# Projecting before the normalisation in two graph convolutions: a column-sum correction for the mean, the row scale in the adjacency matrix

## Chip, core and metric

The kernel runs on one NeuronCore of a Trainium2 chip, in fp32 with some bf16 helpers. The metric is the device time of one launch in microseconds (us), the median of several runs. TensorE is called PE, VectorE DVE, ScalarE ACT, GpSimd POOL and SyncE SP, as in the profile.

## What is computed

Four graph layers on 64 nodes with 768 features and 1024 edges, each added to its input and followed by a LayerNorm over the features. The second and the fourth are the ones that matter here.

```
def _layernorm(x, eps=1e-05):            # over the 768 features of a node
    m = mean(x); v = var(x)
    return (x - m) / sqrt(v + eps)

x = _layernorm(x + L0(x))                # two relational convolutions, each with a gate over 512 query rows
x = _layernorm(x + L1(x))                # GCN:  A @ (x @ W) + b
x = _layernorm(x + L2(x))                # two graph attentions over 3 relations
x = _layernorm(x + L3(x))                # GCN:  A @ relu(A @ (x @ W1) + b1) @ W2 + b2
```

A is the 64x64 normalised adjacency matrix, `norm = dinv[src] * dinv[dst]` summed over the edges and the self-loops.

## The kernel before

The 64x768 node matrix lies as 128x384: the two halves of the features on two halves of the partitions. So a tile such as `xa`, `t0`, `t1`, `hx` is one node matrix, `gcnT` (128x128) holds A transposed twice on the diagonal, and a 768x768 weight is `W[slot]`, 6 blocks of 128 rows, loaded by SP in a fixed order with `load(key, dram, semaphore, value)`. A product with a node matrix needs it turned: PE turns `xa` block by block into PSUM (`turn_nodes`, `turn_group`), with `gcnT` as the right side, which multiplies by A at the same time, DVE copies the result to `nodeT` (`block_out`, line 864), and PE multiplies `nodeT` with the weight (`project_wide`, line 1194) in two column parts of 256 and 128. Each product of a part is issued for two halves that lie side by side in the array, a pair.

LayerNorm (`layer_norm`, lines 876 to 889) is a chain over three engines: DVE makes `bn_stats` of three blocks (L874) and `bn_aggr` (L878), PE averages over the two partition halves with the matrix `avg` (L1540), DVE makes the variance (L881, L882), ACT the square root (L749), DVE the reciprocal (L886) and then the normalised `xa` in two pieces (L888). While DVE and ACT are at it PE runs filler products, `keep_warm` (L1279), that nobody reads.

Every engine has its own instruction list in program order; semaphores tie them. The order around the change is written out by hand. Before the first LayerNorm the second gate ends: DVE computes `t2 - hh` (L1000), `hh + xa` (L1002), and, once ACT has the gate `alpha` in two parts, `t1 * t2` (L1005) and `t0 = ... + hh` (L1011), each of them with both inputs in SBUF. After the first GCN comes its LayerNorm and the first graph attention: projections L1162 and L1587, the scores, and on DVE a softmax (L1067 leaky relu, L1069 maximum, L1073 masked exponentials with their sum). `v_units` (L1034) are twelve DVE instructions that make a product of a weight of the second attention ahead of time and are fitted into gaps at four places, by the table `V_AT`. POOL (L642) multiplies the tiles of the two gates, its last instruction of weight is the last of these. `L3_W1` is loaded into the slot of `L1_W` once the first GCN's products are done.

## Time and profile before

| | us |
|---|---|
| median of 3 runs | 265.73 (265.25 to 266.22) |
| the profiled execution | 265.27 |
| its span, first to last instruction | 263.4 |
| busy: PE / DVE / ACT / POOL | 249.2 / 156.2 / 96.0 / 84.4 |

The page has busy times by engine, the chain of work that ended last (followed back from the last instruction to whatever released it), and groups of instructions by line. The timeline and the chain of a stretch give single instructions. Times in the rows are us from the start of the span. A busy PE includes the fillers, so its 95% says little on its own; the chain says which of it was waited for.

### The profile page before, as it was taken

To read this page: it belongs to the slowest core of one execution; us is meant where nothing else is said; L and a number is where in the kernel's file an instruction comes from. 1 tells how busy PE (TensorE), PEld (TensorE's weight loads), DVE (VectorE), ACT (ScalarE), POOL (GpSimd) and SP (SyncE) were. 2 spreads that over 40 slices of the span, in tenths; PEclk is the share of its full clock that TensorE was granted. 3 is DMA by queue.
4 is the path that set the end of the run, shared out by engine and by line. 5 is a ranking of instruction groups with operands and counts; after the bars stand their busy time and mean duration, and the time that the engine had idled before them with its cause. 6 is when DMAs were issued, how large, how long until landed. Compare 5 with 4: busy or idle time off the path is not lost.

```text
span 263.4 us, 5173 instructions
## 1 busy us (share of the span) xinstructions
PE 249.2 (95%) x2161; PEld 129.2 (49%) x2161; DVE 156.2 (59%) x281; ACT 96.0 (36%) x159; POOL 84.4 (32%) x78
## 2 busy tenths in 40 slices
PE   8899999998999999899998999999999988999994
PEld 4575654444545542367765333236564443435572
DVE  0745324417887999842926688994767367405322
ACT  2323210008676996313703577871312013013000
POOL 7581000006997799400001768970000000000000
PEclk9999999999999999999999999999999999999999
DMA  6999999899701979340089900005999995000001
GB/s 233 373 402 402 400 325 185 117 366 402 304 1 24 405 290 340 25 119 2 2 298 400 377 6 2 2 0 134 387 404 403 400 341 212 0 0 2 0 2 30
DMA packets 39913, 53.48 MB, mean 203 GB/s; under 512 B 22986, under 2 KB 23754, under 8 KB 39891
## 3 DMA queue, kind: packets, MB, share of 16 engines
q1 hardware_dynamic: 29792, 51.64, 55.2%
q10 hardware_dynamic: 10098, 1.52, 3.4%
q8 instruction: 17, 0.28, 0.4%
q14 instruction: 6, 0.04, 0.0%
HBM read 52.17 MB, written 0.20 MB: 199 GB/s over the span
## 4 chain that ended last, share of the span: by engine, by line
PE 75%; DVE 8%; ACT 6%; DMA 4%; issue 3%; POOL 2%; SPq 1%; DVEq 0%; POOLq 0%
PE ps L1194 12%; PE ps L1310 11%; PE ps L1162 10%; PE ps L1398 7%; PE ps L1209 5%; DMA W<-in_L_gnn_Wg 4%; PE ps L1384 3%; PE ps L1374 3%; PE ps L1279 3%; PE ps L1587 3%; PE ps L1667 3%; PE ps L1138 3%; ACT pre L739 2%; POOL prod L642 2%; PE ps L1455 2%
## 5 line engine op out<-in xcount | busy, mean ns | idle before, releaser
L642 POOL TENSOR_TENSOR prod<-pre,qn 128x768 f32<-128x768 f32 x28 | 54.3, 1956 | 11.2 <-ACT pre L739 11.2
L972 DVE TENSOR_TENSOR pre<-ps,qg 128x768 f32<-128x768 f32 x46 | 43.2, 953 | 11.5 <-PE ps L1384 7.2
L739 ACT ACTIVATE pre<-pre 128x768 f32<-128x768 f32 x46 | 38.5, 848 | 6.5 <-DVE pre L972 6.4
L1310 PE MATMUL ps<-W 128*128 128x384 f32 x96 | 35.2, 492 | 0.7 <-ACT W L479 0.4
L479 ACT COPY W<-ps 128x384 f32<-128x384 f32 x35 | 16.0, 483 | 25.0 <-PE ps L1138 24.9
L1310 PEld LDWEIGHTS ps<-W 128*128 128x128 f32 x96 | 17.1, 190 | 10.3 <-issue 2.2
L1398 PE MATMUL ps<-prod,rsel 128*32 128x384 f32 x192 | 20.5, 497 | 1.3 <-DVE prod L964 0.7
L1194 PE MATMUL ps<-W,prod 128*64 128x256 f32 (+1 forms) x240 | 20.6, 328 | 0.0
L739 ACT ACTIVATE ps<-ps 128x768 f32<-128x768 f32 x18 | 14.2, 795 | 17.2 <-PE ps L1384 16.1
L1194 PEld LDWEIGHTS ps<-W,prod 128*64 128x64 f32 x240 | 15.1, 137 | 4.9 <-issue 0.5
L1138 PE MATMUL ps<-ident,W 128*128 128x128 f32 x108 | 16.6, 280 | 0.8 <-ACT W L479 0.4
L1279 PE MATMUL ps<-bsel 96*128 96x512 bf16 x62 | 16.9, 381 | 0.0
L1138 PEld LDWEIGHTS ps<-ident,W 128*128 128x128 f32 x108 | 13.3, 144 | 6.7 <-issue 3.8
L1162 PE MATMUL ps<-W,prod 128*64 128x384 f32 x96 | 15.6, 486 | 0.0
L964 DVE TENSOR_TENSOR prod<-pre,qn 128x768 f32<-128x768 f32 x12 | 15.5, 1303 | 0.0
L1455 PE MATMUL ps<-stack,bsel 96*128 96x384 bf16 x60 | 14.7, 329 | 0.7 <-ACT W L479 0.7
L628 POOL COPY stack<-hi 32x384 bf16<-32x384 bf16 x2 | 1.2, 610 | 39.6 <-DVE hi L940 39.5
L1162 PE MATMUL ps<-W,nodeT 128*64 128x384 f32 x72 | 12.8, 492 | 0.0
L1194 PE MATMUL ps<-W,nodeT 128*64 128x256 f32 (+1 forms) x144 | 12.7, 328 | 0.0
L1034 DVE CUSTOM_DVE_ANT_0 qn<-W,pre 128x768 bf16<-128x768 f32 x12 | 11.5, 955 | 1.4 <-DVE prod L1034 1.4
L642 POOL TENSOR_TENSOR W<-pre,qn 128x768 f32<-128x768 f32 x6 | 11.0, 1826 | 3.1 <-ACT pre L739 3.1
L1374 PE MATMUL ps<-W,ident_b 64*64 64x384 bf16 x204 | 11.4, 330 | 0.4 <-DVE prod L964 0.4
(248 smaller groups left out, 332.6 us busy)
## 6 DMA issues: line engine op xcount, KB each, us to landing
W<-in_L_gnn_W SPq DMA_DIRECT2D x9, 2304.0 KB, 12.5
W<-in_L_gnn_W_rel SPq DMA_DIRECT2D x6, 2304.0 KB, 17.5
W<-in_L_gnn_W_root SPq DMA_DIRECT2D x2, 2304.0 KB, 16.0
W<-in_L_gnn_Wq SPq DMA_DIRECT2D x4, 1152.0 KB, 9.5
qn<-in_L_gnn_query_embs SPq DMA_DIRECT2D x4, 384.0 KB, 10.1
W<-in_L_gnn_Wg SPq DMA_DIRECT2D x3, 384.0 KB, 3.9
W<-in_L_gnn_Wg SPq DMA_DIRECT2D x1, 1152.0 KB, 9.6
W<-in_L_gnn_Wg SPq DMA_DIRECT2D x12, 96.0 KB, 3.9
```

The source lines that it names most:

```text
L479: ins = nc.vector.tensor_copy(dst, src) if done is turned_out_v else nc.scalar.copy(dst, src)
L642: nc.gpsimd.tensor_tensor(prod_of(T), pre_of(T), qn[:, pair_and_node(t)[0], :], ALU.mult).then_inc(prod_p, 1)
L739: nc.scalar.activation(tile, tile, ACT.Sigmoid).then_inc(sig_ready, 1)
L972: nc.vector.tensor_tensor(dst, ring(T), by_half(qg[:, pair_and_node(T % TILES)[0], :]), ALU.add).then_inc(pre_ready, 1)
L1138: ins = nc.tensor.transpose(ps[:, group_bank(g), at:at + P], src, ident[:, :])
L1162: ins = nc.tensor.matmul(ps[c * N:(c + 1) * N, bank, 0:HD], T[:, j, col0 + h * N:col0 + (h + 1) * N], w[:, k, c * HD:(c + 1) * HD], start= ...
L1194: ins = nc.tensor.matmul(wide(bank)[c * N:(c + 1) * N, cols], T[:, j, col0 + h * N:col0 + (h + 1) * N], w[:, k, c * HD + cols.start:c * HD ...
L1279: nc.tensor.matmul(ps[:, bank, :], bsel[0:3 * GN, 0, :], bsel[0:3 * GN, 0:4, :].rearrange("p a b -> p (a b)"), start=True, stop=True, skip ...
L1310: ins = nc.tensor.matmul(ps[:, unit_bank(u), 0:HD], qT[:, k, p * P:(p + 1) * P], WgT_q[:, k, c * HD:(c + 1) * HD], start=(k == 0), stop=(k ...
L1374: nc.tensor.matmul(ring(T)[to * N:(to + 1) * N, c, :], ident_b[rows, rows], splits[rows, part, c, p, :], start=(part == 0), stop=False)
L1398: ins = nc.tensor.matmul(ps[at:at + GN, ACC, 0:HD], rsel[:, s:s + GN], prod_of(T + g)[:, c * HD:(c + 1) * HD], start=first, stop=last, ski ...
L1455: ins = nc.tensor.matmul(ring(t)[:, c, :], bsel[0:3 * GN, t // 2, :], stack[:, c, t % 2, :], start=True, stop=True)
```

## The change

LayerNorm is linear up to the mean and the scale of a row: with m the mean and r the reciprocal deviation of each node, `A @ ((t - m) r) @ W = (A r) @ (t @ W - m (column sums of W))`. The new kernel turns `t0` as soon as DVE has made its first part, multiplies the unnormalised rows with the weight into two PSUM banks of their own (`project_raw`), takes the mean off with `m * w_cols - raw` on DVE (`take_means`), and multiplies with `gcnS = -r * gcnT` on PE (`times_adj`). The column sums come in two steps: POOL adds the six row blocks of the weight (`sum_rows`, five instructions of 128x768), PE multiplies the result with ones (`sum_weights`), ACT copies it out (`sums_out`).

For the last convolution, ACT first copies PSUM to `t1`, since the rows to be turned must be in SBUF. The norm itself is still made, for the residual. V_AT goes from 3, 3, 4, 2 to 0, 4, 4, 4.

```diff
-        V_AT = (3, 3, 4, len(V_UNITS) - 10)
+        V_AT = (0, 4, 4, len(V_UNITS) - 8)
@@ SP
-            load("L3_W1", a["L3_gnn_W1"], proj_done, 2)
+            sp.wait_ge(w_summed, 1)
+            load("L3_W1", a["L3_gnn_W1"], raw_done, 2)
@@ POOL
+            def sum_rows(key):
+                wait_loaded(pool, key)
+                w = W[SLOT[key]]
+                link(nc.gpsimd.tensor_tensor(w_rows, w[:, 0, :], w[:, 1, :], ALU.add))
+                for k in range(2, KC - 1):
+                    link(nc.gpsimd.tensor_tensor(w_rows, w_rows, w[:, k, :], ALU.add))
+                nc.gpsimd.tensor_tensor(w_rows, w_rows, w[:, KC - 1, :], ALU.add).then_inc(w_summed, 1)
+
+            pool.wait_ge(prod_p, pool_tiles(2 * TILES))
+            sum_rows("L1_W")
             pool.wait_ge(reduced, TILES)
             nc.gpsimd.memset(V_f, 0.0).then_inc(v_cleared, 1)
+            pool.wait_ge(w_sums_done, 1)
+            sum_rows("L3_W1")
@@ ACT
+            def sums_out(i):
+                act.wait_ge(w_sums_done, i + 1)
+                nc.scalar.copy(w_cols[i], ps[:, SUM_BANK, 0:HD]).then_inc(w_sums_out, 1)
...
+            for part, cols in enumerate(PARTS_OF):
+                act.wait_ge(att_part, part + 1)
+                nc.scalar.copy(t1[:, cols], wide(RGAT2)[:, cols]).then_inc(y_made, 1)
             ln(3)
+            sums_out(1)
@@ DVE
                 nc.vector.bn_aggr(small[:, 0:2], small[:, 20:20 + 6 * JC]).then_inc(ln_parts, 1)
+                if turned_n is not None:
+                    block_out(nodeT, node_turned, nodeT_ready, turned_n, 2, 1)
...
+                if turned_n is not None:
+                    nc.vector.tensor_scalar(gcnS, gcnT[:, :], small[:, 6:7], -1.0, ALU.mult, ALU.mult).then_inc(gcn_scaled, 1)
...
-                        link(nc.vector.tensor_tensor(t0[:, cols], t1[:, cols], hh[:, cols], ALU.add))
+                        nc.vector.tensor_tensor(t0[:, cols], t1[:, cols], hh[:, cols], ALU.add).then_inc(x_made, 1)
+                        dve.wait_ge(x_made, i + 1)
                         stats(t0[:, :], i)
+                        if i == 0:
+                            block_out(nodeT, node_turned, nodeT_ready, 3, 2, 0)
...
+            def take_means(i):
+                dve.wait_ge(w_sums_out, i + 1)
+                for part, cols in enumerate(PARTS_OF):
+                    dve.wait_ge(raw_done, 2 * i + part + 1)
+                    nc.vector.scalar_tensor_tensor(out=raw[:, cols], in0=w_cols[i][:, cols], scalar=small[:, 2:3],
+                                                   in1=raw_psum(part), op0=ALU.mult, op1=ALU.subtract).then_inc(raw_ready, 1)
@@ PE
-                keep_warm(1 if layer == 0 else 10, 4)
+                keep_warm(1, 4)
...
+            def project_before_norm(y, made, n, key, turned_n):
+                w = W[SLOT[key]]
+                turn_group(y, ident, node_turned, (made, 1), 2, 0)
+                keep_warm(1, 4)
+                wait_loaded(pe, key)
+                pe.wait_ge(nodeT_ready, 2 * turned_n - 1)
+                project_raw(w, 0, BY_BLOCK[:2])
+                turn_group(y, ident, node_turned, (made, 1), 2, 1)
+                pe.wait_ge(ln_parts, n)
+                nc.tensor.matmul(ps[:, MEANS, 0:2], avg[:, :], small[:, 0:2], start=True, stop=True).then_inc(ln_mean, 1)
+                project_raw(w, 0, BY_BLOCK[2:4])
+                sum_weights(n // 2)
+                pe.wait_ge(nodeT_ready, 2 * turned_n)
+                project_raw(w, 0, BY_BLOCK[4:]).then_inc(raw_done, 1)
+                project_raw(w, 1).then_inc(raw_done, 1)
+
+            def times_adj(i, part):
+                if part == 0:
+                    pe.wait_ge(gcn_scaled, i + 1)
+                pe.wait_ge(raw_ready, 2 * i + part + 1)
+                cols = PARTS_OF[part]
+                nc.tensor.matmul(wide(GCN)[:, cols], gcnS, raw[:, cols], start=False, stop=True,
+                                 skip_group_check=True).then_inc(proj_done, 1)
```

On PE the place behind the second gate reads, before (t is `t0`, L1540 the mean, L1265 the turning with `gcnT`, L1236 adding `xa`, L1194 the projection):

```order
L1279 MATMUL ps<-bsel 128x512 x10
L1540 MATMUL ps<-small,avg 128x2 [waits ln_parts]
L1217 MATMUL ps<-biases,i 64x256 x2
L1217 MATMUL ps<-biases,i 64x128 x2
L1279 MATMUL ps<-bsel 128x512 x4
L1265 MATMUL ps<-gcnT,xa 128x128 [waits x_ready] x2
L1265 MATMUL ps<-gcnT,xa 128x128
L1236 MATMUL ps<-xa,ident 64x256 x2
L1236 MATMUL ps<-xa,ident 64x128 x2
L1194 MATMUL ps<-W,nodeT 64x256 [waits nodeT_ready,L1_W_0_loaded]
...
L1194 MATMUL ps<-W,nodeT 64x128 x12
```

and now (L1305 turns `t0`, L1614 is the raw projection, L1623 the column sums, L1650 the product with the scaled matrix):

```order
L1305 MATMUL ps<-ident,t 128x128 [waits x_made,alpha_ready]
...
L1339 MATMUL ps<-bsel 128x512
L1614 MATMUL ps<-W,nodeT 64x256 [waits nodeT_ready,L1_W_0_loaded]
...
L1305 MATMUL ps<-ident,t 128x128 [waits x_made]
L1637 MATMUL ps<-small,avg 128x2 [waits ln_parts]
L1614 MATMUL ps<-W,nodeT 64x256 x4
L1623 MATMUL ps<-pre,small 64x384 [waits w_summed]
...
L1614 MATMUL ps<-W,nodeT 64x128 x12
...
L1296 MATMUL ps<-xa,ident 64x256 [waits x_ready]
...
L1650 MATMUL ps<-prod 128x256 [waits raw_ready,gcn_scaled]
L1650 MATMUL ps<-prod 128x128 [waits raw_ready]
```

The projection has moved ahead of every wait on the norm but that on `ln_parts`; the norm is waited for at L1296 and L1650 alone.

At the end of POOL's list, before (L642 is the gates' product, L646 the memset of `V_f`):

```order
L642 TENSOR_TENSOR prod<-pre,qn 128x768 [waits reduced,sig_ready] x2
L642 TENSOR_TENSOR W<-pre,qn 128x768 [waits reduced,sig_ready] x2
L642 TENSOR_TENSOR prod<-pre,qn 128x768 [waits reduced,sig_ready] x2
L646 MEMSET prod 128x192 [waits reduced]
L48 UNCONDITIONAL_BRANCH
```

and now (L658 the gates' product, L665 to L668 the sums of the weight's row blocks, L673 the memset):

```order
L658 TENSOR_TENSOR prod<-pre,qn 128x768 [waits reduced,sig_ready] x2
L665 TENSOR_TENSOR pre<-W 128x768 [waits L1_W_0_loaded,prod_p]
L667 TENSOR_TENSOR pre<-pre,W 128x768 [waits pool_chain] x3
L668 TENSOR_TENSOR pre<-pre,W 128x768 [waits pool_chain]
L673 MEMSET prod 128x192 [waits reduced]
L665 TENSOR_TENSOR pre<-W 128x768 [waits L3_W1_0_loaded,w_sums_done]
L667 TENSOR_TENSOR pre<-pre,W 128x768 [waits pool_chain] x3
L668 TENSOR_TENSOR pre<-pre,W 128x768 [waits pool_chain]
L48 UNCONDITIONAL_BRANCH
```

Ten instructions of the gates' form are new, five free to start right after the last product, five once `L3_W1` has landed; the memset stands behind the first five.

On ACT at the last convolution, before (L788 copies a part of the attention's projection, L749 is the square root):

```order
L786 COPY qg<-ps 64x128 [waits wts_turned]
L788 COPY qn<-ps 64x384 [waits rel_done]
L749 ACT_TABLE_LOAD
L749 ACTIVATE small<-small 128x1 [waits ln_var] x2
L792 DMA out<-t 64x384 [waits x_ready]
```

and now (L824 a square root for its table's sake, L827 the copy to `t1`, L778 the square root, L782 the column sums):

```order
L823 COPY qn<-ps 64x384 [waits rel_done]
L824 ACT_TABLE_LOAD
L824 ACTIVATE small<-small 128x1
L827 COPY t<-ps 128x256 [waits att_part]
L827 COPY t<-ps 128x128 [waits att_part]
L778 ACTIVATE small<-small 128x1 [waits ln_var]
L782 COPY pre<-ps 128x384 [waits w_sums_done]
L778 ACTIVATE small<-small 128x1 [waits ln_var]
```

The copies to `t1`, for which DVE's statistics and PE's turning wait, stand behind the table load.

## Rows read from the trace of the kernel before

**Rows 1.** The page: chain that ended last by engine, and the granted clock's row.

```profile
PE 75%; DVE 8%; ACT 6%; DMA 4%; issue 3%; POOL 2%; SPq 1%; DVEq 0%; POOLq 0%
...
core 0: 263.4 us, clock 0.998
```

**Rows 2.** The chain, around the first convolution: start us, duration us, what.

```profile
185.40 2.26 PE ps L1279 x10
...
191.17 3.90 PE ps L1194 x48
195.07 1.19 PE ps L1279 x5
...
196.41 0.17 DVE small L881
```

**Rows 3.** Timeline, DVE at the end of the second gate: start us, duration us, instruction.

```profile
180.85 0.55 DVE L1000 TENSOR_TENSOR t<-t,hh 128x384 f32<-128x384 f32 x1
...
181.44 0.56 DVE L1002 TENSOR_TENSOR hh<-hh,xa 128x384 f32<-128x384 f32 x1
...
184.62 0.43 DVE L1005 TENSOR_TENSOR t<-t 128x256 f32<-128x256 f32 x1 [2.63 <-ACT t L745]
...
185.09 0.42 DVE L1011 TENSOR_TENSOR t<-t,hh 128x256 f32<-128x256 f32 x1
```

**Rows 4.** Timeline, POOL: the last product of the gates.

```profile
174.48 1.83 POOL L642 TENSOR_TENSOR prod<-pre,qn 128x768 f32<-128x768 f32 x1 [0.20 <-ACT pre L739]
```

**Rows 5.** Timeline, first gate: POOL and DVE products side by side.

```profile
89.38 1.83 POOL L642 TENSOR_TENSOR prod<-pre,qn 128x768 f32<-128x768 f32 x1
...
90.43 1.60 DVE L964 TENSOR_TENSOR prod<-pre,qn 128x768 f32<-128x768 f32 x1
...
93.68 1.83 POOL L642 TENSOR_TENSOR prod<-pre,qn 128x768 f32<-128x768 f32 x1
...
94.94 1.39 DVE L964 TENSOR_TENSOR prod<-pre,qn 128x768 f32<-128x768 f32 x1
...
95.69 2.32 POOL L642 TENSOR_TENSOR prod<-pre,qn 128x768 f32<-128x768 f32 x1 [0.18 <-ACT pre L739]
```

**Rows 6.** Groups by line, DVE: busy us, mean ns; one input in PSUM.

```profile
L964 DVE TENSOR_TENSOR W<-ps,qn 128x768 f32<-128x768 f32 x10 | 9.5, 950 | 0.0
```

**Rows 7.** SP's issue of L3_W1 (start, duration), and its time to landing.

```profile
195.11 2.92 SPq L508 DMA_DIRECT2D W<-in_L_gnn_W  x1
...
W<-in_L_gnn_W SPq DMA_DIRECT2D x1, 2304.0 KB, 20.6
```

**Rows 8.** The chain in the softmax of the first attention.

```profile
216.70 0.37 DVE qg L1067
...
217.45 0.28 DVE qg L1067
...
218.62 0.36 DVE qg L1073
...
219.70 1.92 PE ps L1651 x16
```

**Rows 9.** Timeline, last convolution.

```profile
241.63 1.28 ACT L749 ACT_TABLE_LOAD   x1
...
242.70 0.96 DVE L874 BATCH_NORM_STATS2 small<-ps 128x6 f32<-128x128 f32 x3 [1.10 <-PE ps L1692]
...
250.08 0.42 DVE L1127 TENSOR_SCALAR hx<-ps 128x256 f32<-128x256 f32 x1 [2.54 <-PE ps L1194]
...
252.78 1.47 PE L1194 MATMUL ps<-W,prod 128*64 128x256 f32 x12
```

**Rows 10.** Timeline, the V units and what PE wants behind them.

```profile
199.18 0.95 DVE L1034 CUSTOM_DVE_ANT_0 qn<-W,pre 128x768 bf16<-128x768 f32 x1
...
204.90 0.58 PE L1594 MATMUL ps<-ident,qn 64*128 64x64 f32 x6
...
224.37 0.95 DVE L1034 CUSTOM_DVE_ANT_0 qn<-W,pre 128x768 bf16<-128x768 f32 x1
...
229.44 0.55 PE L1676 MATMUL ps<-ident,qn 128*128 128x128 f32 x3
```

More of the change, by code:

```diff
@@ L140, in gnn_kernel @@
         vscratch = qn_f[:, 2 * D + KC * R * N:2 * D + KC * R * N + HD].bitcast(BF16)
+        w_rows = pre[:, 2, :]
+        w_cols = [pre[:, 3, i * HD:(i + 1) * HD] for i in range(2)]
+        raw = prod[:, 0, 0:HD]
+        gcnS = prod[:, 1, 0:P]
         score = qg_f[:, 0:HD]
@@ L162, in gnn_kernel @@
         CUT = 2 * P
+        RAW_BANKS = (2, 1)
+        SUM_BANK = 5
         PARTS_OF = (slice(0, CUT), slice(CUT, HD))
@@ L256, in gnn_kernel @@
         x_ready = sem("x_ready")
+        x_made = sem("x_made")
+        y_made = sem("y_made")
+        w_summed = sem("w_summed")
+        w_sums_done = sem("w_sums_done")
+        w_sums_out = sem("w_sums_out")
+        raw_done = sem("raw_done")
+        raw_ready = sem("raw_ready")
+        gcn_scaled = sem("gcn_scaled")
         ln_parts = sem("ln_parts")
@@ L583, in _ @@
             nc.gpsimd.memset(small[:, 41:42], LN_EPS)
+            nc.gpsimd.memset(small[:, 45:46], 1.0)
             pool.wait_ge(ident_ready, 1)
@@ L1010, in _, with raw_psum @@
                     else:
-                        link(nc.vector.tensor_tensor(t0[:, cols], t1[:, cols], hh[:, cols], ALU.add))
+                        nc.vector.tensor_tensor(t0[:, cols], t1[:, cols], hh[:, cols], ALU.add).then_inc(x_made, 1)
+                        dve.wait_ge(x_made, i + 1)
                         stats(t0[:, :], i)
-            layer_norm(t0[:, :], xa[:, :], 1)
+                        if i == 0:
+                            block_out(nodeT, node_turned, nodeT_ready, 3, 2, 0)
+            layer_norm(t0[:, :], xa[:, :], 1, 3)
+            def raw_psum(part):
+                return ps[:, RAW_BANKS[part], 0:(CUT if part == 0 else HD - CUT)]
+            def take_means(i):
[4 more added lines that the diff above has]
+                                                   in1=raw_psum(part), op0=ALU.mult, op1=ALU.subtract).then_inc(raw_ready, 1)
+            take_means(0)
             def projection_norm(y, dst, n, done):
@@ L1543, in norm_stats, with raw_psum, project_raw @@
                 keep_warm(4, SPARE)
-            norm_stats(1, "L1_gnn_b")
-            turn_nodes(xa, gcnT, node_turned, made=(x_ready, 2))
+            def raw_psum(part):
+                return ps[:, RAW_BANKS[part], 0:(CUT if part == 0 else HD - CUT)]
+            def project_raw(w, part, chunks=BY_BLOCK):
+                cols = PARTS_OF[part]
+                for k in chunks:
+                    h, j = k // JC, k % JC
+                    for c in range(2):
+                        ins = nc.tensor.matmul(raw_psum(part)[c * N:(c + 1) * N, :], nodeT[:, j, h * N:(h + 1) * N],
+                                               w[:, k, c * HD + cols.start:c * HD + cols.stop],
+                                               start=(k == 0), stop=(k == BY_BLOCK[-1]), skip_group_check=True)
+                return ins
@@ new lines, in sum_weights @@
+            def sum_weights(i):
+                pe.wait_ge(w_summed, i + 1)
+                for c in range(2):
+                    ins = nc.tensor.matmul(ps[c * N:(c + 1) * N, SUM_BANK, 0:HD], small[:, 45:46].to_broadcast([P, N]),
+                                           w_rows[:, c * HD:(c + 1) * HD], start=True, stop=True, skip_group_check=True)
+                ins.then_inc(w_sums_done, 1)
+            def project_before_norm(y, made, n, key, turned_n):
[13 more added lines that the diff above has]
+                project_raw(w, 1).then_inc(raw_done, 1)
@@ L1547, in _ @@
+            pe.wait_ge(x_ready, 4)
             add_nodes_wide(xa, GCN)
-            wait_loaded(pe, "L1_W")
-            project_wide(nodeT, W[SLOT["L1_W"]], GCN, (0,), first=False, waits=as_copied(nodeT_ready, 3)).then_inc(proj_done, 1)
-            project_wide(nodeT, W[SLOT["L1_W"]], GCN, (1,), first=False).then_inc(proj_done, 1)
+            for part in range(2):
+                times_adj(0, part)
             norm_stats(2)
@@ L1747, in _ @@
                 attend(wT2, X2, part, True).then_inc(att_part, 1)
-            norm_stats(3, "L3_gnn_b1")
-            turn_nodes(xa, gcnT, node_turned, made=(x_ready, 5))
-            keep_warm(1, SPARE)
-            wait_loaded(pe, "L3_W1")
-            project_wide(nodeT, W[SLOT["L3_W1"]], GCN, (0,), first=False, waits=as_copied(nodeT_ready, 6)).then_inc(proj_done, 1)
-            project_wide(nodeT, W[SLOT["L3_W1"]], GCN, (1,), first=False, chunks=BY_BLOCK[:4])
+            project_before_norm(t1, y_made, 3, "L3_W1", 6)
+            add_bias_wide("L3_gnn_b1", GCN)
+            for part in range(2):
+                times_adj(1, part)
+            add_bias_wide("L3_gnn_b2", LAST)
+            pe.wait_ge(x_ready, 10)
+            add_nodes_wide(xa, LAST)
             turn_group(hx, gcnT, node_turned, (y_ready, 1), 2, 0)
-            project_wide(nodeT, W[SLOT["L3_W1"]], GCN, (1,), first=False, chunks=BY_BLOCK[4:]).then_inc(proj_done, 1)
-            add_bias_wide("L3_gnn_b2", LAST)
-            add_nodes_wide(xa, LAST)
             wait_loaded(pe, "L3_W2")
```

22 lines of the change are left out of this document (15 added, 7 removed).

## The prediction, made before the changed kernel ran

> **What bounds the kernel now.** I read the page's chain of work first: three quarters of the span are TensorE (PE) instructions that follow one another, and the engines named beside it stand in the chain only where a stage hands over [rows 1]. The change touches two such hand-overs: the first graph convolution behind the gates (L1, around 180 to 197 us) and the first of the last two (L3, around 241 to 253 us). In the chain of the first [rows 2] the reader sees PE's last alpha projection end at 185.40, ten filler products (keep_warm), then, after VectorE (DVE) and ScalarE (ACT) have made the norm, the projection L1194 from 191.17 to 195.07, and the next norm's first DVE instruction at 196.41. Nothing of value runs on PE from 185.4 to 191. That hole is what the change aims at, by running the projection on the unnormalised rows.
>
> Then I looked at who else is awake. GpSimd (POOL) has its last product at 174.48 and is free from 176.31 on [rows 4]. The change gives it ten new instructions, and what these meet on DVE decides the case.
>
> **Part 1: the first convolution, taken by itself.** Columns price all the fp32 products: the 24 products of L1194 are 6 pairs of 384 columns in 3.90 us, so 0.65 a pair [rows 2]. After the change PE starts as soon as the first half of t0 exists. L1011 ends at 185.51 [rows 3]; two bn_stats of 0.32 [rows 9] bring DVE to 186.2, two transposes (three take 0.55 [rows 10]) are in by then, the 256-column copy costs 0.42 like every DVE instruction of that width [rows 3], so the first raw product can start at 186.8. From there PE is serial: projection 3.90, column sums of the weight 0.65, adding xa 0.65, the product with the scaled adjacency matrix 0.65, bias 0.17 (a bf16 filler of 512 columns is 0.23 [rows 2]), transpose and mean 0.4, and 0.2 of waiting for bn_aggr, which the block copy put between the two halves of the statistics has pushed back: 6.6. End at 193.4 against 195.0. DVE's own tail (scaling gcnT, the two norm halves, two scalar_tensor_tensor) is done before PE needs it. Since both parts of the last product now come within 0.2 us, bn_stats of part 0 no longer hides: 0.2 to 0.3 back. So **minus 1.3 us** for this stage if nothing disturbs it. The table load for the square root stands right behind the sigmoid, as before.
>
> **Part 2: GpSimd's sums of the weight rows.** Five tensor_tensor of 128x768 fp32 for each weight, both inputs in SBUF, chained. The same form took 1.83 [rows 4], so 9.2 us plus gaps of some 0.07. The first five run from 176.4 to about 186.2; PE asks for their result only at about 189: hidden as to PE. The question is DVE, and the trace answers it. Where a DVE tensor_tensor with both inputs in SBUF (0.95 alone) starts inside a POOL tensor_tensor, it doesn't share, it waits [rows 5]: POOL's runs from 89.38 to 91.21, DVE's starts at 90.43 and takes 1.60, that is 0.65 more, the 0.78 left of POOL's instruction less 0.13. POOL's from 93.68 to 95.51: DVE's starts at 94.94 with 0.57 left and takes 0.44 more. In return POOL's next, at 95.69, takes 2.32 instead of 1.83, until DVE has ended at 96.33. DVE instructions with one input in PSUM keep 0.95 beside a busy POOL [rows 6]. So two such streams alternate: one DVE instruction of any length for each POOL instruction of 1.83. The Trainium skill states this as a rule ("SBUF — State Buffer", section "Who interferes with whom": DVE and GpSimd share a pair of SBUF ports, a DVE instruction with two SBUF inputs contends for it, and the one that comes second is blocked until the other has ended). It speaks against this change, and by that rule, with which the rows above agree within 0.02 us, the sum is the one worked out below; by a proportional sharing it would be that of rival (a).
>
> In the first convolution the four DVE instructions with two SBUF inputs are L1000, L1002, L1005, L1011 [rows 3]. Laid against POOL's instructions (third one 180.18 to 182.01, and so on): L1000 ends at 182.43, L1002 at 184.55, L1005 starts at 184.60 inside POOL's fifth (184.19 to 186.24) and ends at 186.54, L1011 at 187.0 instead of 185.51. That is 1.5 us at the head of the stage, and all behind it is serial: PE ends at 194.9, the next norm starts 0.2 later than before. Part 1 with it: **plus 0.2** (minus 1.3, plus 1.5). The bounds of this term are minus 1.3 (no blocking) and plus 0.7 (POOL's fifth instruction falling a further 0.5 later).
>
> The second five wait for L3_W1. SyncE issues that load at 195.11 and it lands 20.6 us later, at 215.7 [rows 7]. The change lets it be issued at raw_done 2, about 193.4, but the DMA engines are full (five weights in a row), so I keep 215.7, and 214.5 as the early end. From then on POOL wants some 9.5 us, and DVE stands in the softmax of the first graph attention, which is a pure latency chain [rows 8]: L1067 (one SBUF tensor read twice, by two inputs), L1067, L1073, L1073, with PE's L1651 waiting at 219.70. The walk, shifted by 0.2: the first L1067 at 216.9 inside POOL's first, ends 217.8 (0.6 late); the second at 218.15 inside POOL's second, ends 219.7 (1.8 late); the first L1073 ends 221.6; the second starts 221.9 inside POOL's fourth and ends 223.6 instead of 219.0. **Plus 4.6 us.** POOL's fifth then lies beside PSUM copies, save for a tensor_scalar of 128x2 (0 to 0.6 more). If the weight lands at 214.5, the same walk gives 5.5; if only the two L1073 were blocked, 2.5; if sharing were proportional (twice the time for the streamed part), about 0.6; without contention 0.
>
> **Part 3: the last convolution.** Before, statistics read PSUM at 242.70. Now ACT copies to t1 first, and its table load, at 241.63 for 1.28, stands ahead of that copy [rows 9], with a dummy sqrt of 0.2: copy from 243.15 to 243.5, 0.85 us late. Here DVE has POOL to itself, since the sums are long done. Walk: first half copied at 244.65, raw products from 244.7; the mean product, put behind two of them and a transpose, answers at 246.3, so the row scale comes at 247.1 (before: 245.4); raw products end at 249.7, both products with the scaled matrix at 250.6. The relu of part 0, at 250.08 before [rows 9], comes at 250.55. But bias and xa now precede the turning of hx where they stood behind it, so the last weight's products start at 252.8, against 252.78 [rows 9]. **0.0 us**, bounds minus 0.4 and plus 0.4: the two cancel by what stands in front of one copy.
>
> **Part 4: moved work.** The V units (L1034, 1.14 from one to the next) go from 3, 3, 4, 2 to 0, 4, 4, 4. The four of the second place start at 199.2 and end at 203.7, and PE wants what DVE copies behind them (0.56) at 204.90; the four of the last start at 224.37, end at 228.8, the copy at 229.4, PE wants it at 229.44 [rows 10]. Covered both times, the last by under 0.1 us. SyncE's new wait on w_summed (186.2) is over before raw_done. Removed fillers cost nothing here, PE has work in their place. The V_f memset moves behind POOL's sums, to about 186, and its first reader is now at 199.
>
> **Sum.** The profiled execution took 265.27 us, 1.87 more than its span of 263.4. 265.27 + 0.2 + 4.6 + 0.0 = 270.1. The median of the three runs is 0.46 above that execution, so 270.5.
>
> **Rivals.**
> (a) *No or weak blocking of these forms* (add in place of multiply, narrow DVE instructions); it decides if a narrow instruction waits less than about 0.3 us: minus 1.3, 0 to plus 0.6 in the softmax, 0 in the last: 264.0 to 265.1, by the median 264.4 to 265.5. For it: rows 5 show one form of 768 columns only, the softmax instructions have 192. Against: what is waited for there is POOL's instruction, not DVE's width.
> (b) *Only part blocks*: the two L1073 or only one stage: 266.5 to 268.5. This is where a POOL start that happens to fall well ends too.
> (c) *The clock falls*: in the blocked softmax PE has its fillers done at about 218.3 and then only transposes until 223.8, while in the trace of before it hardly stands still and the mean granted clock is 0.998 [rows 1]. At 1.2 instead of 2.4 GHz the 1.92 us of L1651 [rows 8] and some 1.5 us of transposes and first products behind it would double: plus 1 to 3.4, 271.5 to 274. This rival ends further on the slower side; it decides only once the blocking is there.
>
> **How the numbers follow.** Blocking in both places as walked, 0.58 (269.3 to 271.5 by the median); (c) on top of it 0.10; (b) 0.14; (a) 0.18, of which about 0.12 is more than 0.3% below 265.73 and 0.06 within it. A change of 0.3% (0.8 us) is about what a measurement of this kernel can tell from none. (b) spreads a little below 266.5, 0.02 of it. So slower 0.80, within 0.08, faster 0.12. The range leaves out (a) and the far end of (c): 266.4 to 272.4.
>
> **What would show it.** In the profile after: POOL ten instructions of 1.83 or, where they waited, up to 2.3 us, the first at 176.4, the sixth at about 215.7; L1000's successor taking 1.5 and not 0.55, L1005's 1.9; the projection's PE block ending near 195 (near 193.4 under (a)); L1067 and L1073 of 0.35 us taking 0.9 to 1.7; PE idle ahead of the transposes of the weights; the mean granted clock (below 1 under (c)); the last weight's products starting 10.7 us before the end of the span as now. The prediction is wrong if the narrow DVE instructions keep their 0.35 beside a busy POOL, or if the weight lands so late that POOL meets only PSUM copies.

## Result: slower by 3.7%, beyond the range of the prediction

| | before | after |
|---|---|---|
| median, us | 265.50 (265.25 to 266.22) | 275.44 (273.69 to 276.82) |
| ratio | | 1.037 [1.032, 1.042] |
| the profiled execution, us | 265.27 | 273.69 |
| its span, us | 263.4 | 271.9 |
| mean granted clock | 0.998 | 0.974 |

The forecast was 270.5, from 266.4 to 272.4. The medians here are over four executions each, the profiled one among them. The ratios below leave out three executions that lie far off the rest (271.34 of the kernel before, 603.77 of d_narrow, 604.14 of k_memsets).

From the page after, the busy times and the clock's row (tenths of full speed, 6.8 us a slice):

```profile
PE 251.2 (92%) x2150; PEld 129.3 (48%) x2150; DVE 166.0 (61%) x287; ACT 97.9 (36%) x165; POOL 103.2 (38%) x89
...
PEclk9999999999999999999999999999999965799999
```

DVE's busy time is up by 9.8 us (156.2 before) with six instructions more (281 before), and the clock has a hole at slices 33 to 35. The timeline of the first convolution, POOL and DVE, answers [rows 3, 4] (L1044, L1046, L1049 and L1055 are L1000, L1002, L1005 and L1011 of before; L923 is L881):

```profile
176.38 1.82 POOL L665 TENSOR_TENSOR pre<-W 128x768 f32<-128x768 f32 x1
178.28 5.81 POOL L667 TENSOR_TENSOR pre<-pre,W 128x768 f32<-128x768 f32 x3
184.16 2.00 POOL L668 TENSOR_TENSOR pre<-pre,W 128x768 f32<-128x768 f32 x1
...
180.84 1.57 DVE L1044 TENSOR_TENSOR t<-t,hh 128x384 f32<-128x384 f32 x1
182.45 2.05 DVE L1046 TENSOR_TENSOR hh<-hh,xa 128x384 f32<-128x384 f32 x1
184.62 1.83 DVE L1049 TENSOR_TENSOR t<-t 128x256 f32<-128x256 f32 x1
186.48 0.42 DVE L1055 TENSOR_TENSOR t<-t,hh 128x256 f32<-128x256 f32 x1
...
196.66 0.16 DVE L923 TENSOR_TENSOR small<-small,ps 128x1 f32<-128x1 f32 x1 [0.48 <-PE ps L1600]
```

The walk had L1044 end at 182.43 (it did at 182.41), L1046 at 184.55 (184.50), L1049 at 186.54 (186.45), L1055 at 187.0 (186.90). The next norm stands at 196.66 against 196.41 [rows 2]: 0.25 late, where 0.2 was forecast. Now the softmax (L1126 is L1067, L1132 is L1073 [rows 8]; L1137 adds a constant to two columns, L1747 turns the weights on PE):

```profile
215.07 1.81 POOL L665 TENSOR_TENSOR pre<-W 128x768 f32<-128x768 f32 x1 [28.71 <-DMA W<-in_L_gnn_W]
216.96 5.78 POOL L667 TENSOR_TENSOR pre<-pre,W 128x768 f32<-128x768 f32 x3
...
216.96 0.36 DVE L1126 SCALAR_TENSOR_TENSOR qg<-qg 128x192 f32<-128x192 f32 x1
...
217.62 1.58 DVE L1126 SCALAR_TENSOR_TENSOR qg<-qg 128x192 f32<-128x192 f32 x1
...
219.50 1.58 DVE L1132 CUSTOM_DVE_ANT_0 qg<-qg,M 128x192 f32<-128x192 f32 x1
...
221.01 1.95 DVE L1132 CUSTOM_DVE_ANT_0 qg<-qg,M 128x192 f32<-128x192 f32 x1
...
224.03 0.62 DVE L1137 TENSOR_SCALAR small<-small 128x2 f32<-128x2 f32 x1
...
217.29 1.04 PE L1339 MATMUL ps<-bsel 96*128 96x512 bf16 x4
...
223.02 0.48 PE L1747 MATMUL ps<-ident,qg 128*128 128x128 f32 x1 [1.20 <-DVE small L1132]
...
224.07 3.41 PE L1760 MATMUL ps<-qn,qg 128*64 128x192 f32 x16
...
225.94 0.42 DVE L1145 SCALAR_TENSOR_TENSOR t<-ps,small,t 128x192 f32<-128x192 f32 x1 [0.51 <-PE ps L1760]
```

DVE's narrow instructions wait for POOL's wide ones. Only the first L1126 got through: it started at 216.96, in the gap between POOL's first and second addition. PE meanwhile is out of fillers from 218.3. Busy time by stretch (busy us and records of PE, PEld, DVE, ACT, POOL, then the granted clock, the share of the DMA engines and GB/s):

```profile
218.00:220.00 2.00, 0.32 (x2) 0.00 (x0) 1.97 (x3) 0.57 (x2) 1.92 (x2) 1.00 1.03 409
220.00:222.00 2.00, 0.69 (x2) 0.23 (x2) 2.00 (x3) 0.21 (x2) 1.92 (x2) 0.55 0.35 139
222.00:232.00 10.00, 8.98 (x33) 3.32 (x35) 6.73 (x18) 1.27 (x5) 2.55 (x2) 0.50 0.01 2
...
234.00:236.00 2.00, 2.00 (x14) 0.84 (x12) 0.88 (x2) 0.00 (x0) 0.00 (x0) 1.00 0.00 0
```

PE was busy for 0.32 of two microseconds; then the granted clock is 0.50, its lower level of 1.2 GHz, up to about 233.7, and back at 1.00 from 234. PE's work there takes up to twice as long: four fillers 1.89 (1.04 in the trace of before), the attention's 16 products 3.41 (1.97 there). Last, the end of the second attention and the last convolution, on PE, DVE and ACT, against [rows 9, 10]:

```profile
237.43 0.55 PE L1785 MATMUL ps<-ident,qn 128*128 128x128 f32 x3
...
248.85 0.29 DVE L1175 COPY qg<-ps 128x128 f32<-128x128 f32 x1 [0.53 <-PE ps L1847]
...
249.63 1.28 ACT L824 ACT_TABLE_LOAD   x1
...
251.14 0.54 ACT L827 COPY t<-ps 128x256 f32<-128x256 f32 x2
...
252.77 1.08 PE L1614 MATMUL ps<-W,nodeT 128*64 128x256 f32 x8 [0.55 <-DVE nodeT L904]
...
258.16 0.92 PE L1650 MATMUL ps<-prod 128*128 128x256 f32 x4
...
261.27 1.51 PE L1254 MATMUL ps<-W,prod 128*64 128x256 f32 x12 [0.61 <-DVE prod L904]
```

PE's L1785 begins 7.99 us later than its counterpart of before [rows 10], the last weight's products 8.49 later [rows 9]: the last convolution has lost 0.5, where 0.0 was forecast.

So the 8.4 us between the two profiled executions lie as follows, each from the lines above:

| where | forecast | trace |
|---|---|---|
| first convolution | +0.2 | +0.25 |
| softmax: the four instructions on DVE, up to the second L1747 at 223.02 (219.05 before) | +4.6 | +3.7 |
| L1137, 0.46 longer (0.16 before), but covered | 0 to +0.6, not in the sum | 0 |
| half clock, from L1747 to L1785 (7.99 less 3.97) | 0 | +4.0 |
| last convolution | 0.0 | +0.5 |

They add up to 8.5. L1137 costs nothing here: DVE's first instruction behind it that needs PE, L1145, still waits 0.51 for the products of L1760, which run at the half clock.

### The profile page after: what moved, and what is told of

Read it like the earlier page. It is cut to its first block, busy times and chain, and to the rows that moved or that the text cites. A ratio compares the mean times of both kernels' runs of the same rounds, so it can differ in the third digit from the quotient of the medians.

```text
span 271.9 us, 5182 instructions
## 1 busy us (share of the span) xinstructions
PE 251.2 (92%) x2150; PEld 129.3 (48%) x2150; DVE 166.0 (61%) x287; ACT 97.9 (36%) x165; POOL 103.2 (38%) x89
## 4 chain that ended last, share of the span: by engine, by line
PE 73%; DVE 10%; ACT 7%; DMA 4%; issue 3%; POOL 2%; SPq 1%; DVEq 0%; POOLq 0%
PE ps L1370 10%; PE ps L1222 9%; PE ps L1254 9%; PE ps L1458 7%; PE ps L1269 4%; PE ps L1776 4%; DMA W<-in_L_gnn_Wg 4%; PE ps L1444 3%; PE ps L1434 3%; PE ps L1614 3%; PE ps L1696 3%; PE ps L1198 3%; PE ps L1339 2%; ACT pre L768 2%; POOL prod L658 2%
## 5 line engine op out<-in xcount | busy, mean ns | idle before, releaser
L658 POOL TENSOR_TENSOR prod<-pre,qn 128x768 f32<-128x768 f32 x28 | 54.4, 1957 | 11.2 <-ACT pre L768 11.1
L665 POOL TENSOR_TENSOR pre<-W 128x768 f32<-128x768 f32 x2 | 3.6, 1816 | 28.8 <-DMA W<-in_L_gnn_W 28.7
L1339 PE MATMUL ps<-bsel 96*128 96x512 bf16 x41 | 13.4, 417 | 0.0
L650 POOL TENSOR_TENSOR low<-t,mid 128x256 bf16<-128x256 f32 x1 | 0.7, 672 | 32.2 <-DVE mid L991 32.2
L658 POOL TENSOR_TENSOR W<-pre,qn 128x768 f32<-128x768 f32 x6 | 11.0, 1827 | 3.1 <-ACT pre L768 2.9
```

The source lines that it names most:

```text
L658: nc.gpsimd.tensor_tensor(prod_of(T), pre_of(T), qn[:, pair_and_node(t)[0], :], ALU.mult).then_inc(prod_p, 1)
L1339: nc.tensor.matmul(ps[:, bank, :], bsel[0:3 * GN, 0, :], bsel[0:3 * GN, 0:4, :].rearrange("p a b -> p (a b)"), start=True, stop=True, skip ...
```

## Experiments

**The theory** after this reading: (1) POOL's sums block DVE in both places, all else in the change is worth a small gain; (2) PE's idle time in the blocked softmax takes the clock down, and that is the 4.0 us missed; (3) the last convolution costs 0.5 because of what stands ahead of one copy. Rivals: the new order itself costs time; the clock falls for another cause (POOL's or DMA's load); the blocking is not tied to POOL's reading. All ratios below are to runs of the kernel before on the same chip, in brackets the 95% interval.

**The sums taken out of the changed kernel** (a_no_sums). The column sums are left out.

```diff
-                link(nc.gpsimd.tensor_tensor(w_rows, w[:, 0, :], w[:, 1, :], ALU.add))
...
+                nc.gpsimd.memset(w_rows[:, 0:1], 0.0).then_inc(w_summed, 1)
```

> The changed kernel without GpSimd's sums of the weight rows: a memset of one column stands in their place, so the mean correction is computed from a stale tile (part of the computation is left out); every other instruction is that of the changed kernel. Theory (all of the loss comes from those ten GpSimd instructions and what follows from them): no DVE instruction with two SBUF inputs is longer than its 0.3 to 0.6 us, L1049's successor at 185.5, PE's raw block ends near 193.4 to 193.8, the softmax keeps its place, the granted clock is full to the end, and only the last convolution is some 0.5 us longer: 264.3 to 264.9 us, 0.6 to 1.2 below before. Rival (the raw order itself is slower, with its transposes between the products, and the sums only add to it): above 266.

Measured: 264.95 us, ratio 0.998 [0.997, 0.9995], 0.05 above the expected range; the mean clock is 0.994 or more in all twelve executions. DVE in the first convolution and in the softmax:

```profile
181.09 0.55 DVE L1040 TENSOR_TENSOR t<-t,hh 128x384 f32<-128x384 f32 x1
...
184.86 0.42 DVE L1045 TENSOR_TENSOR t<-t 128x256 f32<-128x256 f32 x1 [2.63 <-ACT t L770]
...
217.85 0.36 DVE L1128 CUSTOM_DVE_ANT_0 qg<-qg,M 128x192 f32<-128x192 f32 x1 [0.25 <-ACT qg L798]
```

The durations are those of [rows 3, 8] within 0.01. The rest of the change is worth 0.2%, some 0.5 us; the whole loss is the sums'. The last convolution takes 0.5 longer here too (12.42 from the last copy ahead of it to the last weight's products, 11.92 before; both are worked out below). From the second L1743 to L1781, the counterparts of L1747 and L1785, it is 10.40 us (10.39 before), so the four V units in the last place are covered.

**The sums alone, put into the kernel before** (b_sums_only), with SyncE's wait for them; their result is read by nobody.

```diff
...
+            pool.wait_ge(prod_p, pool_tiles(2 * TILES))
+            sum_rows("L1_W")
             pool.wait_ge(reduced, TILES)
             nc.gpsimd.memset(V_f, 0.0).then_inc(v_cleared, 1)
+            sum_rows("L3_W1")
```

> The kernel before, with nothing added but GpSimd's ten instructions, whose result nobody reads (SyncE waits for the first five before it loads L3_W1, as in the change). Theory: the first five push L1005 and L1011 back by 1.5 us, the second five stretch the softmax by 4 us, PE stands idle there, the clock falls to half for some 14 us: 265.5 + 1.5 + 4.0 + 3.5 to 5 = 274.5 to 276. Rival (GpSimd only costs together with the reordered projection, for instance since the load comes earlier): below 270.

Measured: 275.81 us, 1.040 [1.038, 1.041], inside the expected range and as slow as the whole change (1.037). The projection's order has no part in the loss. In this trace the clock also fell in the first convolution, although all fillers of the kernel before are in place there:

```profile
192.00:194.00 2.00, 2.00 (x13) 1.40 (x14) 1.40 (x4) 0.00 (x0) 0.00 (x0) 0.50 1.05 410
...
222.00:224.00 2.00, 0.00 (x0) 0.00 (x0) 1.97 (x3) 0.45 (x1) 1.92 (x2) 1.00 0.82 332
224.00:234.00 10.00, 8.14 (x31) 3.01 (x33) 6.44 (x18) 1.41 (x5) 2.04 (x3) 0.54 0.01 2
```

**The blocked softmax, with fillers for PE** (c_warm): the changed kernel, 16 fillers in place of 4 ahead of the transposes and 5 between them.

```diff
-                keep_warm(4, ACC)
+                keep_warm(16, ACC)
...
+                    if h == 0:
+                        keep_warm(5, ACC)
```

> The changed kernel with twelve more filler products on PE in front of the wait for the first weights of the softmax and five between the two heads: PE does not stand idle while DVE waits. Theory (clock and waiting are two separate costs, and the clock falls because PE is idle from 218.3 to 221.1): DVE as before at 1.5 to 1.9 us for the three long instructions, the granted clock full throughout, 265.5 + 0.25 + 4.0 + 0.55 = 270.3 us, so 269.5 to 271.5. Rival (the clock falls for another reason, or the fillers end up in the way): 273 to 276 as the changed kernel.

Measured: 271.78 us, 1.023 [1.020, 1.025]: 3.7 us below the changed kernel, with DVE still blocked. The mean clock of the four executions is 0.992 to 1.000.

```profile
217.39 1.29 DVE L1126 SCALAR_TENSOR_TENSOR qg<-qg 128x192 f32<-128x192 f32 x1
...
222.38 1.95 DVE L1132 CUSTOM_DVE_ANT_0 qg<-qg,M 128x192 f32<-128x192 f32 x1
...
224.00:234.00 10.00, 8.51 (x54) 3.66 (x55) 8.24 (x22) 0.98 (x3) 1.91 (x2) 1.00 0.00 0
```

In the trace the clock stays at 1.00 with POOL, DVE and the DMA engines about as busy as in the changed kernel: it was PE's idle time that took it down. The time is 0.3 above the expected range. This time the first L1126 was blocked as well: from its start to the second L1747 (at 224.39) it is 7.00 us, against 6.06 in the changed kernel and 2.35 before, so the softmax loses 4.65 and not 3.7. How much it loses hangs on where POOL's gap falls. At full clock L1137 (0.88) is no longer covered: from L1747 to the counterpart of L1785 (at 235.26) it is 10.87 us, 0.48 more than before. In the changed kernel it is 14.41.

**Narrower sums** (d_narrow): each of the additions split into four of 192 columns.

```diff
...
+                for q in range(4):
+                    at = slice(q * QW, (q + 1) * QW)
+                    link(nc.gpsimd.tensor_tensor(w_rows[:, at], w[:, 0, at], w[:, 1, at], ALU.add))
...
```

> The changed kernel with the same sums cut into four column pieces: 20 instructions of 192 columns for each weight in place of 5 of 768. Theory (a DVE instruction waits for the rest of ONE GpSimd instruction): a piece lasts some 0.5 us, so DVE's instructions with two SBUF inputs wait at most 0.4 each and mostly 0.1 to 0.3; stage one loses 0.4 of its 1.3, the softmax 0.8 to 1.2, PE's idle stretch stays under 2 us and the clock full: 265.0 to 266.6 us. Rival (the two engines share a bandwidth, so the same data cost the same): no change against the changed kernel, 273 to 276.

Measured: 268.13 us, 1.009 [1.0065, 1.011]. The direction holds, the size doesn't. POOL's pieces take 0.59 to 0.60, and DVE's instructions wait for one piece at most:

```profile
176.27 0.59 POOL L667 TENSOR_TENSOR pre<-W 128x192 f32<-128x192 f32 x1
...
216.71 0.59 DVE L1131 SCALAR_TENSOR_TENSOR qg<-qg 128x192 f32<-128x192 f32 x1
...
222.60 0.75 DVE L1154 TENSOR_SCALAR t<-t 128x384 f32<-128x384 f32 x1
...
190.17 0.86 PE L1628 MATMUL ps<-pre,small 128*64 128x384 f32 x4 [0.53 <-POOL pre L669]
...
226.00:228.00 2.00, 2.00 (x10) 0.79 (x8) 1.65 (x5) 0.00 (x0) 1.84 (x3) 0.51 0.00 0
```

Two things were not in my expectation: the sums now end at 190.1, so PE waits for them, and the longer train of POOL pieces still reaches DVE's later instructions (0.75 in place of 0.35), after which PE idles and the clock dips again, for 3 us. Of the five executions that count, the two with a mean clock of 0.998 or more took 267.0 and 267.1, the three with 0.992 or 0.993 took 268.1 to 268.8.

**The second sums placed between the two softmaxes** (e_late).

```diff
             pool.wait_ge(w_sums_done, 1)
+            pool.wait_ge(rel_done, 4)
             sum_rows("L3_W1")
```

> The changed kernel with one more wait: POOL starts the second weight's row sums only when PE has done the fourth relation product, about 228, between the two softmaxes, where DVE has V units and PSUM copies only. Theory (what the second sums cost is where they lie, 4.0 us of blocked softmax and 4.0 us of half clock behind it): the softmax is as before, L1126 0.36 and L1132 0.36, the granted clock stays at 1.00 from 217 to 235, and what is left is +0.25 of the first convolution and +0.5 of the last: 265.9 to 266.6, ratio 1.002 to 1.004. A V unit or two may be blocked (up to 1 us each, PE waits for what stands behind the last one by under 0.1 us), so up to 267.5. Rival (the clock falls from the DMA load or from POOL's work itself, wherever it lies): the clock is at half for some us behind 228 and the time is over 269.

Measured: 268.3 us, 1.010 [1.007, 1.014], in executions that spread from 265.92 (mean granted clock 0.998) to 269.31 (0.987). The softmax is as before and the clock is 1.00 behind it; the fastest execution is the theory's number. But the profiled one, 269.14, shows two other falls, in the first and in the last convolution:

```profile
186.00:189.00 3.00, 1.47 (x11) 0.84 (x11) 2.76 (x9) 1.22 (x2) 0.36 (x2) 0.98 1.02 414
189.00:192.00 3.00, 3.00 (x16) 1.80 (x15) 1.78 (x9) 0.29 (x1) 0.00 (x0) 0.50 1.04 409
...
247.00:250.00 3.00, 3.00 (x17) 1.72 (x15) 0.81 (x5) 0.29 (x1) 0.00 (x0) 0.50 0.00 0
```

Each costs about 1.5 us (3 us at half clock). Neither the expected 265.9 to 266.6 nor the rival as I had put it: the falls are not behind 228, where the sums now lie, but at the two hand-overs where the change took fillers away. In the first of them the missing fillers are not the whole cause: DVE is blocked there too. Without the blocking, PE is busy 2.53 of the 3 us from 186 to 189 with as few fillers, and the clock stays up (a_no_sums).

**The same with fillers at these two places** (l_late_warm): behind the gate's projection, and around the turning of `t0` and `t1`.

```diff
-                keep_warm(1, 4)
+                keep_warm(1 if layer == 0 else 7, 4)
...
+                if n == 3:
+                    keep_warm(3, SPARE)
                 turn_group(y, ident, node_turned, (made, 1), 2, 0)
-                keep_warm(1, 4)
+                keep_warm(3, 4)
```

> e_late (second sums behind 228) with fillers in PE's remaining gaps: seven in place of one behind the second gate's projection, three ahead of the turning of t1, three in place of one behind each first turning. In the trace of e_late the granted clock fell to 0.50 from 189 to 192 and from 247 to 250, each time after PE had stood idle for part of two us. Theory (these two falls, which come in some executions only, are all of what e_late has over 266.2): they are gone, 265.6 to 266.4 with a narrow spread, granted clock 0.995 or more in every execution, though DVE is blocked in the first convolution as before. Rival (the falls come with DVE's or POOL's blocking, or from a budget that PE's work uses up): the clock still falls and the time is 267 or more.

Measured: 266.04 us, 1.002 [1.001, 1.003], no execution with a mean clock under 0.997. So e_late's other 2 us were the clock too. Two of the twelve executions, 266.83 and 266.95, lie above the expected range at a clock of 1.000 and 0.998, for another cause that no run shows.

**The first convolution alone** (h_first_only): the last convolution as before, no second sums.

```diff
             nc.gpsimd.memset(V_f, 0.0).then_inc(v_cleared, 1)
-            pool.wait_ge(w_sums_done, 1)
-            sum_rows("L3_W1")
...
-            project_before_norm(t1, y_made, 3, "L3_W1", 6)
+            norm_stats(3, "L3_gnn_b1")
+            turn_nodes(xa, gcnT, node_turned, made=(x_ready, 5))
...
```

> The changed kernel with the last convolution put back as it was: no second row sums, no copy to t1, the norm first and the projection behind it. The first convolution is as in the changed kernel, with its five additions. Theory: only the +0.25 us of the first convolution is left, 265.4 to 266.1, ratio 0.9995 to 1.003; against the kernel with late sums (e_late) it is 0.3 to 0.7 us faster, which is the price of the last convolution's new order. Rival (the last convolution's order costs nothing and the 0.5 us come from the shorter clock or from chance): the two are within 0.2 us.

Measured: 265.62 us, 1.002 [1.001, 1.004]. Eight of eleven executions lie between 265.28 and 265.77, three near 267.1 with a mean clock of 0.990 or 0.991: a fall of the clock comes in some executions only. That it lies in the first convolution, as in e_late, is not shown, for the profiled execution (265.77) has none. Fastest against fastest, e_late is 0.64 above it (265.92 and 265.28), within the 0.3 to 0.7 expected for the last convolution.

**The same with four additions on POOL** (i_first_four), the sixth row block added by PE.

```diff
+                n_add = KC - 1 if key == "L1_W" else KC
...
-                for k in range(2, KC - 1):
+                for k in range(2, n_add - 1):
...
-                keep_warm(1, 4)
+                if n == 1:
+                    for c in range(2):
+                        nc.tensor.matmul(ps[c * N:(c + 1) * N, SUM_BANK, 0:HD], small[:, 45:46].to_broadcast([P, N]),
+                                         w[:, KC - 1, c * HD:(c + 1) * HD], start=True, stop=False, skip_group_check=True)
```

> h_first_only with four additions on POOL in place of five: POOL adds five row blocks and the sixth is added by PE, which accumulates it in the same bank in the place of one filler product. POOL is then free at 184.1, before alpha lets DVE go on at 184.6. Theory (the first convolution gained 1.3 us by itself, less what two narrow DVE instructions wait for POOL's fifth addition): the products t1*t2 and t0 take 0.43 and 0.42, raw products start at about 187, the next norm 0.8 to 1.0 us earlier than before: 264.4 to 265.0, ratio 0.996 to 0.998. Rival (the stage has no gain in it that a measurement shows): 265.3 to 266.

Measured: 264.24 us (264.04 to 264.54), 0.996 [0.995, 0.997], 0.16 below the expected range: the first version with nothing left out that is faster, by 0.4%. DVE's two wide products are still blocked, but in slack, ahead of `alpha`; the two that count are free, and PE has no gap:

```profile
182.58 2.06 DVE L1040 TENSOR_TENSOR hh<-hh,xa 128x384 f32<-128x384 f32 x1
184.75 0.43 DVE L1043 TENSOR_TENSOR t<-t 128x256 f32<-128x256 f32 x1
...
195.46 0.16 DVE L917 TENSOR_TENSOR small<-small,ps 128x1 f32<-128x1 f32 x1 [0.47 <-PE ps L1593]
...
186.00:189.00 3.00, 3.00 (x23) 1.67 (x25) 2.37 (x10) 1.41 (x3) 0.00 (x0) 1.00 1.03 417
```

The next norm stands at 195.46 where before it stood at 196.41 [rows 2]: 0.95 earlier. One addition less is worth 1.2 us (fastest executions) to 1.4 (medians) against h_first_only.

**All of it, with ACT's table load at two places** (g_best: behind the copies to `t1`; f_late_four: ahead of them, as in the changed kernel). Both have four additions first and late second sums.

```diff
-            nc.scalar.activation(small[:, 47:48], small[:, 41:42], ACT.Sqrt)
             for part, cols in enumerate(PARTS_OF):
                 act.wait_ge(att_part, part + 1)
                 nc.scalar.copy(t1[:, cols], wide(RGAT2)[:, cols]).then_inc(y_made, 1)
+            nc.scalar.activation(small[:, 47:48], small[:, 41:42], ACT.Sqrt)
```

> All of the change, mended: four additions for the first weight as in i_first_four, the second weight's sums behind 228 as in e_late, and ACT's table load for the square root moved behind its two copies to t1. Theory: the first convolution gives -0.9; the last starts 0.5 us earlier than in the changed kernel (copy at 242.65 in place of 243.15 of the walk), which cancels the +0.5 measured there: 264.3 to 265.0, ratio 0.9955 to 0.998, as i_first_four within 0.3. Rival (late table load delays the square root and with it the residual's norm, which PE waits for at the addition of xa): +0.3 to +0.8 against i_first_four.

> g_best with ACT's table load left where the changed kernel has it, ahead of the two copies to t1. Theory: the last convolution alone is 0.4 to 0.6 us slower than in g_best, 264.7 to 265.0, and in executions in which the clock falls at the last convolution (PE stands idle longer ahead of the turning of t1 than in g_best) up to 1.5 us more. Rival (the place of the table load is worth nothing, the +0.5 was the drain of the products with the scaled matrix): within 0.2 us of 264.35.

Measured: g_best 264.35 us, 0.9964 [0.9952, 0.9975]; f_late_four 264.64 us, 0.9964 [0.9952, 0.9976], on another chip. g_best is in its expected range; f_late_four lies between its theory and its rival. The timed runs do not separate them. The traces do, one of each: here the last DVE copy ahead of the attention's product (L1177 in both) and the last weight's first product on PE, of g_best, then of f_late_four:

```profile
239.91 0.29 DVE L1177 COPY qg<-ps 128x128 f32<-128x128 f32 x1 [0.53 <-PE ps L1854]
...
251.79 1.52 PE L1256 MATMUL ps<-W,prod 128*64 128x256 f32 x12 [0.61 <-DVE prod L906]
```

```profile
240.08 0.29 DVE L1177 COPY qg<-ps 128x128 f32<-128x128 f32 x1 [0.53 <-PE ps L1854]
...
252.40 1.51 PE L1256 MATMUL ps<-W,prod 128*64 128x256 f32 x12 [0.61 <-DVE prod L906]
```

From one to the other 11.88 and 12.32 us; in the changed kernel 12.42 (248.85 to 261.27), in a_no_sums the same (240.08 to 252.50), in the kernel before 11.92 (240.86, the copy's start in its timeline, to 252.78 [rows 9]). The new order of the last convolution is worth nothing at best and costs 0.4 to 0.5 with the table load in front. g_best and i_first_four are 0.11 apart: all the gain there is comes from the first convolution.

**POOL writing only** (k_memsets): each addition a memset of the same tile; the column sums are left out.

```diff
...
-                    link(nc.gpsimd.tensor_tensor(w_rows, w_rows, w[:, k, :], ALU.add))
...
+                    link(nc.gpsimd.memset(w_rows, 0.0))
```

> The changed kernel with each of the ten additions replaced by a memset of the same 128x768 tile, so POOL writes SBUF and reads nothing (the column sums are left out). A memset of 128x192 took 0.26 in the trace, so I take some 1.0 us for each. Theory (what blocks DVE is POOL's second input, the reading of two SBUF tensors): DVE's narrow instructions keep 0.55, 0.42 and 0.36, and the time is as without the sums, 264.7 to 265.3. Rival (any POOL instruction on SBUF blocks DVE): DVE's instructions beside the memsets take up to 1 us more, the first convolution is late by nothing (the memsets end before 182.5), the softmax by 1 to 2.5 us, 266 to 268.

Measured: 265.14 us, 0.9995 [0.998, 1.001]. The softmax's masked exponentials, which read two SBUF tensors, beside four memsets:

```profile
217.53 3.12 POOL L666 MEMSET pre<- 128x768 f32 x4 [36.89 <-DMA W<-in_L_gnn_W]
...
217.78 0.36 DVE L1131 CUSTOM_DVE_ANT_0 qg<-qg,M 128x192 f32<-128x192 f32 x1 [0.25 <-ACT qg L801]
```

Not held up: what blocks a DVE instruction with two SBUF inputs is POOL reading SBUF (whether one tensor or two was not run). In the first convolution the memsets were over before DVE's pair began, so this reading rests on the softmax, and mostly on this one instruction. Beside the later memsets two one-input tensor_scalar instructions of 128x192 took 0.38 and 0.31, where they take 0.26 alone.

## Why the prediction was wrong

*The bound and the two hand-overs*: right, but for one reading: from 185.4 to 191 PE is not without work of value. Its turning of `xa` starts at 189.33 in the timeline, and the addition of `xa` follows, so the hole is 3.9 us and not 5.6. The sum does not use it.

*Part 1, the first convolution by itself, minus 1.3*: right in kind, a little large. Unblocked it gives 0.95 (i_first_four), in a kernel whose DVE had got to `alpha`'s product 0.13 later (184.75 against 184.62 [rows 3]); so 1.1 by itself. The column sums took 0.81 and the products with the scaled matrix 0.92, where columns gave 0.65 each.

*Part 2, blocking*: right, and the step the readers should keep. Each wait was the rest of POOL's instruction, for 192 columns as for 768. First convolution 0.25 for 0.2, closer than its parts: the wait at its head was 0.1 smaller than forecast (1.4 for 1.5, 186.90 for 187.0) and the gain 0.2 smaller, and the two errors cancel by luck. Softmax 3.7 for 4.6: I let the shift of 0.2 count twice, and the weight landed so that the first L1126 slipped through. In c_warm it did not, and the softmax lost 4.65, where the walk without the double shift has 4.4. By the Trainium skill ("SBUF — State Buffer", section "Who interferes with whom") a DVE instruction with two SBUF inputs contends with a GpSimd instruction that reads SBUF and not with one that only writes it; the traces agree, with 1.58 beside the additions and 0.36 beside the memsets.

*Part 3, the last convolution, 0.0*: mis-sized by 0.5. The walk up to the first raw product was met (copy, statistics and raw start are where it put them, shifted by 7.99); the two groups of raw products that stand by themselves took 1.08 each, where columns gave 0.87, and the products with the scaled matrix 0.92 for 0.65, so the last weight came at 253.3 on the scale of before and not at 252.8. Moving the table load behind the copies takes it back (11.88 us, 11.92 before).

*Part 4, moved work*: nothing seen against it. With all of it in, a_no_sums has the stretch of the last V units at 10.40 us (10.39 before); no run varies V_AT alone.

*Rival (c), the clock*: **this is the step that failed.** I had named the cause, the place and PE's idle time, and then gave it a chance of 0.10 and a price of 1 to 3.4 us. The sum put nothing for it, and the range left out its far end. Given the blocking it happened in all four executions (mean clock 0.968 to 0.975) and cost 4.0 us in the profiled one, since the clock stayed at 0.50 for some 13 us, well past the attention's products by which I priced it: four fillers (1.89 us for 1.04) ran in it too, and so did most of 32 products of the next projection (7.02 for 5.38). The sum had 270.1 for the profiled execution; with 0.9 less in the softmax, 4.0 for the clock and 0.5 for the last convolution it is 273.7 (273.69 measured). The rest of the miss is that the median lies 1.75 above that execution, not 0.46: the other three executions were 1.3 to 3.1 us slower still. Two of them (275.87 and 276.82) have a mean clock of 0.968, by which a further fall of some 3 us at half clock, as e_late shows it at the first and the last convolution, would fit. The third (275.02) has 0.975, no lower than the profiled one, so its 1.3 us are not the clock; a blocked first L1126, as in c_warm, would fit. No trace of those three exists, so this is argued and not shown.

*Rivals (a) and (b)* are out: the trace shows narrow instructions of 192 and 256 columns blocked, and in both places, and in a_no_sums they are not.

What stays open: why the clock falls at the first convolution in some executions and not in others, at the same idle time of PE. From 186 to 189 PE was busy 1.47 us in e_late's trace, where it fell, and 1.46 in the changed kernel's and 1.20 in h_first_only's, where it did not.

## What to carry to other kernels

Before work is given to an idle GpSimd, list the VectorE instructions with two SBUF inputs, and the one-input tensor_scalar instructions, that will meet it: each, however narrow, may wait for a whole GpSimd instruction, so GpSimd's place in time matters more than its load (10 us lost, or 1 us gained, with nearly the same instructions). Where a wait is added in front of TensorE, count the idle time that it leaves there and keep fillers in it; a gap much longer than those of the trace before is to be priced as a fall of the clock, over all of TensorE's work until the clock is back. Fillers that a change makes "useless" can have been what held the clock: with them put back, e_late's falls were gone (l_late_warm).

## What was new about the hardware

- The blocking holds for the smallest instructions: a one-input tensor_scalar of two columns (0.16 alone) took 0.62 and 0.88 beside a GpSimd addition, one of 384 columns 0.75 in place of 0.35. So it is not only the two-input instructions that wait.
- After PE had been busy 0.32 of 2 us the granted clock stood at 0.50 for about 13 us, though PE was 90% busy in it. After smaller gaps it stood there for about 3 us (e_late, d_narrow), and in b_sums_only, where PE did nothing for two whole microseconds, for about 10.
- GpSimd's addition of 192 columns takes 0.59, of 768 columns 1.82. Four pieces cost 0.5 us more than one; by an estimate from these two widths, 0.18 of each instruction does not depend on the width.
